# Half of a PSUM weighing moved from VectorE to ScalarE and GpSimd, in the FFN of a vision tower

## The reference

```python
x = queries.reshape(-1, D)                     # 12672 tokens of 128, after a layernorm
q = (x @ Wq + bq).reshape(-1, N_HEADS, D_KEYS)
s1 = einsum('bhc,hnc->bhn', q1, keys[:, 0]); s2 = ...   # 8 heads, 2 sides, 64 keys
s1t, i1 = top_k(s1, 8); s2t, i2 = top_k(s2, 8)
scores, best = top_k(all 64 sums of s1t and s2t, 8)
inner = einsum('bd,bhkd->bhk', x, w_down[indices])      # 64 of 4096 rows for a token
vals = relu(inner) * softmax(scores)
out = einsum('bhk,bhkd->bd', vals, w_up[indices])
```

## Time and profile before

| what | value |
|---|---|
| median of three runs | 8454.49 us (8449.08 to 8458.87) |
| the profiled execution, its time | 8431.05 us |
| its span | 8426.6 us |
| VectorE busy | 6795.1 us (81%) |
| TensorE busy | 6782.0 us (80%) |
| ScalarE busy | 3191.5 us (38%) |
| GpSimd busy | 1868.7 us (22%) |

### The profile page before, as it was taken

One profiled execution on the slowest core, in us unless ns is written; L12 is line 12 of the kernel. 1 busy time (PEld: TensorE's weight loads), 2 busy tenths in 40 slices (PEclk: granted clock), 3 DMA queues, 4 the chain that ended last, 5 costly groups with the idle time before them and its releaser, 6 DMA issues. The chain is left out here.

```text
span 8426.6 us, 214041 instructions
## 1 busy us (share of the span) xinstructions
PE 6782.0 (80%) x81626; PEld 5204.1 (62%) x81626; DVE 6795.1 (81%) x24876; ACT 3191.5 (38%) x6847; POOL 1868.7 (22%) x2305
## 2 busy tenths in 40 slices
PE   8788888888888888835777777768888888888888
PEld 8566666666666666624555555547677677766776
DVE  2666666666666666668999999969999999999998
ACT  0444444444444444424555555522222222222221
POOL 0222222222222222223444444410000000000000
PEclk9899888888888888867888888879999999999998
DMA  6333333333333333300000000010000000000000
GB/s 195 53 47 47 47 50 48 48 48 52 48 46 45 48 47 44 48 13 5 5 4 4 5 4 4 5 33 9 10 10 8 10 10 10 8 10 10 10 8 8
DMA packets 335682, 245.80 MB, mean 29 GB/s; under 512 B 36150, under 2 KB 333401, under 8 KB 334332
## 3 DMA queue, kind: packets, MB, share of 16 engines
q1 hardware_dynamic: 334716, 232.82, 16.4%
HBM read 61.50 MB, written 13.04 MB: 9 GB/s over the span
## 5 line engine op out<-in xcount | busy, mean ns | idle before, releaser
L585 DVE TENSOR_REDUCE negmax<-S 99x4 f32<-99x788 f32 x1024 | 1001.3, 978 | 1038.0 <-PE S L352 1025.4
L471 ACT ACTIVATE probs<-ST 99x792 f32<-99x792 f32 x1024 | 851.2, 831 | 1652.3 <-PE ST L362 1651.2
L1388 PE MATMUL f_IN<-f_zT,f_wd 128*128 128x256 f32 x3200 | 880.5, 429 | 0.0
L1388 PEld LDWEIGHTS f_IN<-f_zT,f_wd 128*128 128x128 f32 x3200 | 644.4, 213 | 173.7 <-issue 50.1
L1411 PE MATMUL f_OT<-f_wu,f_act 128*128 128x128 f32 x6400 | 739.3, 277 | 1.4 <-issue 1.4
L1411 PEld LDWEIGHTS f_OT<-f_wu,f_act 128*128 128x128 f32 x6400 | 730.4, 193 | 8.3 <-issue 2.1
L1400 PE MATMUL f_AA<-f_hotp,f_hot 64*128 64x32 bf16 x38400 | 546.1, 174 | 233.1 <-DVE f_act L1656 198.2
L362 PE MATMUL ST<-qs,ks 99*99 99x198 bf16 x4096 | 580.5, 269 | 176.7 <-ACT probs L471 158.4
L352 PE MATMUL S<-ks,qs 96*99 96x198 bf16 x4096 | 578.8, 267 | 177.6 <-DVE negmax L585 150.5
L1462 ACT ACTIVATE f_act<-f_IN 128x512 f32<-128x512 f32 x800 | 478.1, 598 | 637.1 <-PE f_IN L1388 637.1
L1400 PEld LDWEIGHTS f_AA<-f_hotp,f_hot 64*128 64x128 bf16 x38400 | 511.6, 94 | 335.7 <-issue 311.6
(11 more groups left out here) (183 smaller groups left out, 13561.3 us busy)
## 6 DMA issues: line engine op xcount, KB each, us to landing
qs<-parts SPq DMA_DIRECT2D x768, 99.0 KB, 3.6
ks<-parts SPq DMA_DIRECT2D x768, 99.0 KB, 4.5
xbuf<-x_in SPq DMA_DIRECT2D x64, 588.0 KB, 4.4
f_hx<-tokens SPq DMA_DIRECT2D x50, 128.0 KB, 2.2
f_hr<-tokens SPq DMA_DIRECT2D x50, 128.0 KB, 2.1
out<-f_hr SPq DMA_DIRECT2D x50, 128.0 KB, 1.8
qs<-mrows SPq DMA_DIRECT2D x256, 9.3 KB
tokens<-h SPq DMA_DIRECT2D x64, 49.5 KB
```

Source lines behind the costliest of these rows:

```text
L471: A.activation(probs[:, p].rearrange("p h k w -> p h (k w)"), ST[:, :, 0:2 * W], ACT.Exp, scale=float(HD) ** -0.5).then_inc(st_taken, 1)
L585: V.tensor_reduce(negmax[:, j, :, 2 * p:2 * p + 2].rearrange("p q h -> p h q"), S[:, :, 0:2 * W].rearrange("p h (q k) -> p h q k", q=2)[:, ...
L1388: mm = nc.tensor.matmul(IN[k % 2][:, m * STEP:m * STEP + STEP], wd[:, 2 * k + m, :], zT[:, par, :], start=True, stop=True)
```

## The change

VectorE now weighs the first half (c = 0) alone. For the second half ScalarE copies the PSUM bank into a new SBUF tensor `f_aa` (two slots, u % 2), with the elements reordered so that the tokens are innermost, and GpSimd multiplies `f_act` with it in place. Two counts are new: `aa_copied` and `aa_weighed`. TensorE waits for the copy before it writes a bank again, and for all of GpSimd's products before it projects the second half's step. The file's later lines move by up to 26.

```diff
+        aa = sb("f_aa", [128, 2, NP, UNIT])
...
+        aa_copied = Count(sem("f_aa_copied"), UNITS)
+        aa_weighed = Count(sem("f_aa_weighed"), UNITS)
...
@@ tensor, weights(n, u)
                 upto(pe, aa_taken[slot], n, u // 2)
+                if u or not isinstance(n, int) or n > 0:
+                    upto(pe, aa_copied, n, u - 1)
@@ tensor, project(n, par, c), c == 0
                         upto(pe, aa_taken[i], n, aa_taken[i].per)
+                    upto(pe, aa_weighed, n, UNITS)
@@ scalar
+            def copy_weights(n, u):
+                upto(act, aa_ready[u % 2], n, u // 2 + 1)
+                if u or not isinstance(n, int) or n > 0:
+                    upto(act, aa_weighed, n, u - 1)
+                nc.scalar.copy(aa[:, u % 2].rearrange("p n t -> p t n"),
+                               AA[u % 2][1][:].rearrange("p (t n) -> p t n", n=NP)).then_inc(aa_copied.sem, 1)
...
                     normalise(n + 2, par)
+                for u in range(3):
+                    copy_weights(n, u)
+                if has2:
                     copy_z(n + 2, par)
...
                 for u in range(2, UNITS):
+                    if u > 2:
+                        copy_weights(n, u)
                     if has2 and 3 <= u < 7:
@@ vector, weigh(n, par, u)
-                for c in range(2):
-                    sl = act_in[:, par, :, c * TP + t0:c * TP + t0 + UNIT]
-                    last = V.tensor_tensor(sl, sl, AA[slot][c][:].rearrange("p (t n) -> p n t", n=NP), ALU.mult)
-                last.then_inc(aa_taken[slot].sem, 1)
+                sl = act_in[:, par, :, t0:t0 + UNIT]
+                V.tensor_tensor(sl, sl, AA[slot][0][:].rearrange("p (t n) -> p n t", n=NP), ALU.mult
+                                ).then_inc(aa_taken[slot].sem, 1)
@@ gpsimd
+            def weigh(n, par, u):
+                if u == 0:
+                    upto(pool, inner_taken, n, NP // 2)
+                upto(pool, aa_copied, n, u + 1)
+                sl = act_in[:, par, :, TP + u * UNIT:TP + u * UNIT + UNIT]
+                nc.gpsimd.tensor_tensor(sl, sl, aa[:, u % 2], ALU.mult).then_inc(aa_weighed.sem, 1)
...
                     deviations(n + 2)
+                for u in range(UNITS):
+                    weigh(n, par, u)
```

## The result

The changed kernel takes 8487.78 us (median of 7 runs, 8471.77 to 8507.99) against 8449.08 us before (7 runs). The ratio is 1.0048, with a 95% interval of 1.0031 to 1.0065: half a per cent slower, 26 to 55 us. The profiled execution took 8491.29 us.

A forecast was written before the change was run, and what follows sets the result against it. VectorE, nearly full in the FFN, was taken as the bound: 4.2 us a step saved, 4.0 given back, -0.2 over 49 steps is -10 us, giving 8421 us from the profiled execution (8445 by the median); range 8230 to 8530.

The forecast's parts named there:

- The mechanism: FFN stage: VectorE's gain from fewer weighings is given back waiting for GpSimd's products; net -0.2 us a step, chance 0.47.
- the upper bound, 1.05 us: Most that one GpSimd product can hold up VectorE: 1.27 us less its fixed part 0.22; the lower bound was nothing.
- The first rival: VectorE isn't held up by GpSimd, so 3.6 to 4.8 us a step stays saved: about 8250 us, chance 0.28.
- The saving: Eight of sixteen PSUM weighings a step leave VectorE, 0.60 us each: 3.6 to 4.8 us a step, taken as 4.2.
- Four meetings, 4.0 us a step: GpSimd's products of units 1, 2, 4 and 6 each hold up VectorE by 0.9 to 1.05 us.
- Unit 7: short operations: VectorE runs only short operations beside GpSimd's product of unit 7, so no meeting and no cost there.
- phase A: Step's first part, columns to unit 1's product, about 22 us; VectorE and TensorE equally long; two weighings there, 1.2 us, uncertain.
- phase B: Remaining 34.5 us of a step, set by VectorE; six weighings there count fully, 3.6 us, and all four meetings fall there.
- The second rival: GpSimd's product takes 1.8 us because of runs of 16: +2.2 us a step, +108 us, 8560 us; chance 0.21.
- The cover: ScalarE's eight copies, 5.0 us a step, fall where ScalarE would wait for TensorE: price nothing, at most 8 x 0.62 us.
- What would show it: Expected profile: GpSimd products 1.1 to 1.4 us free, up to 3.6 waiting; VectorE instructions about 1 us late; step 56 us.

## Why the prediction was wrong

**The mechanism was right.** The gain on VectorE is given back at GpSimd, in meetings of whole instructions. The rows of before showed it for GpSimd's side; for VectorE's side I took the upper bound, 1.05 us, and the longest f_hotp is 1.06 us late. No row had shown that bound: it was argued, and it held. GpSimd's product was put at 1.27 us and takes 1.25 to 1.28. The rule of the Trainium skill that I weighed (SBUF — State Buffer, section SBUF: two separate sides) holds for VectorE's side too: by it VectorE waits for the whole instruction that came first, and f_hotp and f_hot do. As I put the rule, it names VectorE operations with two SBUF inputs; L1615, which has one, is held up as well. The first rival, about 8250 us, is what the kernel without products does (8254).

**The saving was right.** 4.2 us a step was taken between 3.6 and 4.8; the kernel without copies and products measures 4.15. The middle was a choice between two bounds, so the fit to 0.05 us is luck.

**The step that failed is "Four meetings, 4.0 us a step".** What was given back is 5.10 us. It divides as follows, by the groups above and by VectorE's waits in the changed kernel and in the one without products.
- The four meetings that I placed, at the units 1, 2, 4 and 6 (f_hotp, f_hotc, f_hot, f_pick and f_half): 186 us, 3.8 us a step. Here the sum was 0.2 too high, since they don't come in every step.
- A fifth meeting, at unit 7: about 41 us, 0.8 us a step, of which 29 are L1615's. The prediction has "Unit 7: short operations" among those with "None". L1615 is a bitwise and of integers with one SBUF operand: 220 ns by its mean before, 1276 ns by its median after. I had tested the short operations by their length and not by what they are held up by; an instruction of 0.2 us can stand for 1.1 us as well as one of 2.3. A few short ones beside unit 5 add 0.1.
- TensorE: 0.4 us a step. Of VectorE's waits for it, 0.9 us a step more than before, 0.5 stand in the kernel without products too, and are part of what keeps the saving at 4.15 and not 4.8. The other 0.4 come with the meetings (16.7 us by the lines above, 19 inside the 49 steps). I had put phase A's share into the saving, and had not asked what VectorE's lateness in phase B does to it. TensorE idles 3.2 us a step before the columns, against 2.5 before and 1.2 without products (157.8, 127.2 and 57.9 us in 50 steps); the twelve inner matmuls behind them take 3.93 us on the mean against 3.37 without products, counted in the two traces; and the mean granted clock is 0.92 against 0.95 (5700 to 8100 us; 0.93 before). That the longer idle time is what lowers the clock is argued from these numbers; no run changes it alone.

3.8 + 0.8 + 0.1 + 0.4 is the 5.1.

**The second rival had the sign.** It was slower "as soon as the held part is over 1.05 us, or with a fifth meeting". The held part was as forecast; the fifth meeting came. I gave it the price of a longer product, 8560 us, and no price to the fifth meeting alone: -0.2 + 1.05 us a step is +42 us by its own terms, and +46 us was measured in the steps. That these are so near is in part luck: the five meetings are worth 4.6 us and not 5.05, and what TensorE adds makes up for it.

**ScalarE's copy was mis-sized without effect.** 0.62 us was taken for the reordered write and 1.04 us is what it takes. The cover held: with one row on GpSimd all eight copies cost nothing. The longer copy does start each product 0.4 us later, and so has a say in which instruction it meets.

**What would show it** was partly right: GpSimd's waiting products of 2.8 us, f_hotp, f_hot and f_pick 1 us longer. The step of 56 us was wrong, at 57.3. TensorE's idle time before the columns, put near 3 us for the forecast, is 3.2 us on the mean.

## What to carry to other kernels

Work moved from VectorE to GpSimd is free only while VectorE is in instructions that don't need what GpSimd needs; list VectorE's instructions behind each start of a GpSimd one, the short ones too, and count every one that can be held. Each costs about the length of the GpSimd instruction less 0.2 us, whatever its own. If the moved work has slack, gate its start on the end of VectorE's last instruction of the holding kind: here, with six of the eight units moved, this made 0.9980 into 0.9826. And put the units that lie where another engine sets the pace last in the count: unit 0 alone saved nothing, and all three of phase A's gave 1.3 of 1.8 us.

## What the runs showed of the hardware

- VectorE instructions that were held up: operations on two SBUF operands in bf16 (f_hotp, f_hot, f_hotc, f_pick) and in f32 (f_ex, a mean of 346 ns where it was 284), and also some with one SBUF operand: the integer operation L1615 (up to 1323 ns where 220 is its mean before) and casts such as L1618. The weighing L1673, whose second operand is in PSUM, was not (mean 703 ns, and 702 in the kernel without products), nor were the searches.

```profile
L1618 DVE CAST f_gotf<-f_goti x50: 219/221/1322, 5616.0 to 8424.1; 128x128 f32<-128x128 uint32 x50
```

- ScalarE's copy of 128x512 f32 from PSUM takes 0.585 us when it writes in order and 1.04 us when neighbouring elements go 16 apart.
- GpSimd's product of the same size takes at least 1.25 us with f_act in runs of 16 elements and f_aa in order, and 1.48 us when f_aa is read with a stride of 32.
- Access changes hands between GpSimd's instructions too: cut in two, a product holds f_hotp up by 0.51 us at most and not by 1.06.
